# A two-layer local-attention block around full attention, one core: first weights loaded and split by q, k and v, clears moved from POOL to DVE, masks in two steps, q's rearranging read issued before k's writes have landed, and the order of all steps laid out from other numbers

## The reference

```python
x = L0_attn_x
x = x + 0.5 * _L0_ffn_ref(_layernorm(x), ...)   # 2 layers, local attention, 8 heads of 64, window 64
x = x + _L0_attn_ref(_layernorm(x), ...)        # causal attention, 16 heads of 8
x = x + 0.5 * _L0_ffn_ref(_layernorm(x), ...)   # the same two layers and weights again
```

## Time and profile before

| | us |
|---|---|
| median of 3 runs | 1801.35 |
| lowest and highest run | 1790.93 and 1801.44 |
| the profiled execution's own time | 1793.28 |
| its span, first to last instruction | 1791.4 |
| its mean granted TensorE clock, as a share of 2.4 GHz | 0.948 |

### The profile page before, as it was taken

One profiled execution on the slowest core, in us unless ns is written; L12 is line 12 of the kernel. 1 busy time (PEld: TensorE's weight loads), 2 busy tenths in 40 slices (PEclk: granted clock), 3 DMA queues, 4 the chain that ended last, 5 costly groups with the idle time before them and its releaser, 6 DMA issues.

```text
span 1791.4 us, 48412 instructions
## 1 busy us (share of the span) xinstructions
PE 1562.1 (87%) x17754; PEld 1259.1 (70%) x17754; DVE 1448.5 (81%) x2953; ACT 1311.4 (73%) x3846; POOL 1303.5 (73%) x1562
## 2 busy tenths in 40 slices
PE   3789799898988899887989899998889988898987
PEld 3667677666767777766767777776667777677776
DVE  6778789777877889877887998886788897687895
ACT  2588687667677888686779886766578877587885
POOL 7899857368648988687699997732489785469891
PEclk9799999889989999998999998997899999799999
DMA  5001101202010111111010111020210101100000
GB/s 154 16 20 28 42 23 49 92 11 60 13 49 19 25 30 49 33 25 51 24 27 19 25 27 49 21 91 26 71 26 19 52 19 55 51 22 22 19 23 13
DMA packets 49346, 66.75 MB, mean 37 GB/s; under 512 B 8114, under 2 KB 32220, under 8 KB 49116
## 3 DMA queue, kind: packets, MB, share of 16 engines
q1 hardware_dynamic: 49116, 63.66, 12.6%
...
## 4 chain that ended last, share of the span: by engine, by line
POOL 30%; DVE 22%; PE 21%; ACT 11%; DMA 7%; issue 7%; SPq 2%; POOLq 0%; ACTq 0%; DVEq 0%
POOL sums L1198 10%; POOL parts L1188 8%; POOL parts L1202 7%; ACT probs L1264 6%; DVE parts L1568 6%; DMA laid_dram<-halves 4%; PE bank L1640 4%; PE bank L1827 3%; DVE neg_full L1447 3%; DMA stacked_k<-laid_dram 3%; PE bank L1690 2%; PE bank L1788 2%; DVE sums L1575 2%; PE bank L1872 2%; POOL sums L1195 2%
## 5 line engine op out<-in xcount | busy, mean ns | idle before, releaser
L1188 POOL TENSOR_TENSOR parts<-parts 128x256 f32<-128x256 f32 x512 | 382.6, 772 | 136.2 <-DVE parts L1568 134.8
L1198 POOL TENSOR_TENSOR sums<-sums,neg_half 128x8 f32<-128x8 f32 x256 | 434.3, 1696 | 21.3
L1264 ACT ACTIVATE probs<-bank,neg_max 128x128 f32<-128x128 f32 x1024 | 366.2, 406 | 56.4 <-DVE neg_max L1447 54.5
L1568 DVE TENSOR_TENSOR parts<-bank,rope 128x1024 f32<-128x1024 f32 x256 | 309.0, 1216 | 48.3 <-ACT squares L1322 46.7
L1202 POOL TENSOR_TENSOR parts<-parts,sums 128x512 f32<-128x512 f32 x256 | 280.1, 1094 | 37.3 <-POOL sums L1198 0.9
L1264 ACT ACTIVATION_READ_ACCUMULATOR probs<-bank,neg_max 128x1 f32 x1024 | 249.9, 246 | 0.0
L1872 PE MATMUL bank<-ident,parts 128*128 128x128 f32 x1024 | 163.9, 284 | 67.2 <-POOL parts L1202 64.5
L1322 ACT ACTIVATE squares<-bank 128x512 f32<-128x512 f32 x256 | 158.8, 624 | 64.3 <-PE bank L1640 39.2
L1872 PEld LDWEIGHTS bank<-ident,parts 128*128 128x128 f32 x1024 | 117.4, 144 | 99.8 <-issue 71.8
L1640 PE MATMUL bank<-wqkv_hi,h_hi 128*128 128x512 f32 x384 | 179.3, 467 | 4.0 <-ACT q_t L1340 0.8
L1447 DVE TENSOR_REDUCE neg_max<-bank 128x4 f32<-128x512 f32 x256 | 164.2, 681 | 20.6 <-PE bank L1711 19.9
...
## 6 DMA issues: line engine op xcount, KB each, us to landing
between<-val SPq DMA_DIRECT2D x192, 128.0 KB, 2.3
...
stacked_q<-laid_dram SPq DMA_DIRECT2D x16, 512.0 KB, 3.2
stacked_k<-laid_dram SPq DMA_DIRECT2D x16, 512.0 KB, 4.3
...
```

The lines of the kernel that those rows point to most:

```text
L1188: last = nc.gpsimd.tensor_tensor(joined[:, :, dst], joined[:, :, dst], sines[:, :, src], ALU.add)
L1198: nc.gpsimd.tensor_tensor(sums[:, u], sums[:, u], neg_half[:], ALU.pow).then_inc(sems["pool_step"], 1)
L1264: last = nc.scalar.activation(probs[:, u, block:block + wide].rearrange("p b j -> p (b j)"), bank[:, at:at + P * wide], ACT.Exp, bias=neg_ ...
L1568: nc.vector.tensor_tensor(parts[:, u].rearrange("p o (h d) -> p o h d", d=LOCAL_D), bank[:].rearrange("p (o h d) -> p o h d", o=1, d=LOCAL ...
```

## The change

What is computed stays the same. Eight things differ:

- The first projection's weights come as three DMAs (q, k and v columns, `load_qkv`), each with a semaphore; q's stands second in SP's queue, ahead of x of stream 1 and the table. The splits are made for q, k and v apart (512 columns each, for both layers), and `weights_of` lets a `Q` step wait for its own piece only.
- The clears and the ones go from POOL to DVE, ahead of DVE's first statistics; 17 instructions in all, `state`'s old 8 clears aside.
- `MASKS` is two steps: the local masks (the step that stands first) and the full masks, which only full `S` waits for.
- `write` sends q's three DMAs first and then k's, with a semaphore for each, and `lay` issues q's read when q's three have landed, and k's read when k's have.
- The model's durations are changed by some hundredths to a few tenths, `SPREADING` from 9.5 to 14.5 and `WRITING` from 3.6 to 7.5.
- The tables of due times hold other numbers, and a new table `NUDGE` moves single steps.
- Hence each engine's order is another one from the first rows on.
- In that order, ACT's table of functions is loaded 96 times instead of 102.

```diff
-PIECES = [("qkv_hi", 0), ("qkv_lo", 0), ("table", 0), ("w1_scaled", 0), ("w1_hi", 0), ("w1_lo", 0), ("qkv_hi", 1),
-          ("qkv_lo", 1), ("table", 1), ("w1_scaled", 1), ("w1_hi", 1), ("w1_lo", 1), ("wf_scaled", 0), ("wf_hi", 0),
-          ("wf_lo", 0)]
+QKV = ("q", "k", "v")
+PIECES = [(f"{x}_{half}", 0) for x in QKV for half in ("hi", "lo")] + [("table", 0)] + [
+    (f"w1_{x}", 0) for x in ("scaled", "hi", "lo")] + [(f"{x}_{half}", 1) for x in QKV for half in ("hi", "lo")] + [
+    ("table", 1)] + [(f"w1_{x}", 1) for x in ("scaled", "hi", "lo")] + [(f"wf_{x}", 0) for x in ("scaled", "hi", "lo")]
...
-    "SPLIT": [(DVE, 0.85)], "WO": [(PE, 1.75), (DVE, 0.88)],
+    "SPLIT": [(DVE, 0.87)], "WO": [(PE, 1.65), (DVE, 0.88)],
...
-WRITING = 3.6
-SPREADING = 9.5
...
+WRITING = 7.5
+SPREADING = 14.5
...
+STRETCH = 2.1968
+PATIENCE = (0.0, 0.0, 0.144, 0.715)
...
-BEGIN = (1.5, 2.0, 1.0, 5.3)
...
+BEGIN = (2.0, 2.0, 4.5, 1.7)
...
-        return [(POOL, 5.4)]
+        return [(POOL, 3.8 if n else 5.4)]
...
-        return made(("qkv_hi", l), ("qkv_lo", l))
+        x = "v" if kind == "VAL" else QKV[n % 2]
+        return made((f"{x}_hi", l), (f"{x}_lo", l))
...
-                    wait(x, 0, masks)
+                    wait(x, 0, masks[1])
...
-        entry_loaded = sem("entry_loaded")
+        entry_loaded = [sem(f"{x}_loaded") for x in QKV]
...
-        WRITES = 16 * 2 * len(PARTS)
+        WRITES = 16 * len(PARTS)
...
+            def load_qkv(m):
+                sp.dma_start(raw_qkv[:, 0, INNER * m:INNER * (m + 1)],
+                             a["L0_ffn_wqkv"][0, :, INNER * m:INNER * (m + 1)]).then_inc(entry_loaded[m], 16)
+
             load_x(0)
+            load_qkv(0)
+            load_x(1)
             with nc.allow_non_contiguous_dma(reason="bias columns, once"):
 
-                sp.dma_start(rope[:, 1], a["rope"].rearrange("(t p) a b d -> p t a b d", p=P)).then_inc(entry_loaded, 16)
-                sp.dma_start(raw_qkv[:, 0], a["L0_ffn_wqkv"][0]).then_inc(entry_loaded, 16)
+                sp.dma_start(rope[:, 1], a["rope"].rearrange("(t p) a b d -> p t a b d", p=P)).then_inc(scales_loaded, 16)
                 for m, name in enumerate(("L0_ffn_q_scale", "L0_ffn_k_scale")):
                     for l in range(LAYERS):
 
                         src = a[name][l:l + 1].to_broadcast([P, LOCAL_D])
                         sp.dma_start(qk_scale[:, m, l], src).then_inc(scales_loaded, 16)
-                for s in range(1, STREAMS):
+                load_qkv(1)
+                load_qkv(2)
...
-                for part, of in enumerate(PARTS):
-                    for w in range(2):
-                        sp.dma_start(laid[u, w, :, part], halves[SET_OF[step[1:3]]][:, of[w]].bitcast(F32)).then_inc(written[u], 16)
+                for w in range(2):
+                    for part, of in enumerate(PARTS):
+                        sp.dma_start(laid[u, w, :, part], halves[SET_OF[step[1:3]]][:, of[w]].bitcast(F32)).then_inc(written[u][w], 16)
 
             def lay(step):
 
                 u, nth, k = SPREAD_OF[("QF",) + step[1:]], SPREAD_NTH[step[1:]], SET_OF[step[1:3]]
-                sp.wait_ge(written[u], WRITES * nth)
                 sp.wait_ge(spread_pads, 16 * 2 * SPREADS)
                 for w, dst in enumerate((stacked_q, stacked_k)):
+                    sp.wait_ge(written[u][w], WRITES * nth)
...
-            for k in range(SETS):
-                nc.gpsimd.memset(between[k][0:HALF, 0], 0.0)
-            nc.gpsimd.memset(val_full[:], 0.0)
-            nc.gpsimd.memset(spaced[:], 0.0)
-            nc.gpsimd.memset(pads[:], 0.0).then_inc(cleared, 1)
-            n += 1
-            pool.wait_ge(cleared, n)
-            for j in range(P // PAD_D):
-                nc.gpsimd.memset(pads[PAD_D * j:PAD_D * j + 2 * CHUNKS, 1], 1.0).then_inc(cleared, 1)
-                n += 1
-                pool.wait_ge(cleared, n)
-            for k in range(VALUES_FULL):
-                for t in range(TILES):
-                    ones = val_full[:, k, t, 0:FULL_HEADS * VAL_D].rearrange("p (h d) -> p h d", d=VAL_D)[:, :, FULL_D:VAL_D]
-                    last = nc.gpsimd.memset(ones, 1.0)
-            last.then_inc(pads_cleared, 1)
...
+            def make_masks_full():
+                nonlocal n
+                nc.gpsimd.memset(mask_full[:], 0.0)
+                nc.gpsimd.memset(mask_turned[:], 0.0).then_inc(cleared, 1)
+                n += 1
+                pool.wait_ge(cleared, n)
+                for rows in (slice(0, HALF), slice(HALF, P)):
+                    for half in range(2):
+                        select(mask_full[rows, half:half + 1], HALF * half, -1, 1, ALU.is_ge, MASKED)
+                        select(mask_turned[rows, half:half + 1], -HALF * half, 1, -1, ALU.is_ge, MASKED)
+                nc.gpsimd.memset(pool_mark[:], 0.0).then_inc(sems["masked"], 1)
...
-                if what == "qkv_hi":
+                if what[0] in QKV:
+                    x = QKV.index(what[0])
+                    cols = slice(INNER * x, INNER * (x + 1))
+                if what in ("q_hi", "k_hi", "v_hi"):
                     if m == 0:
-                        dve.wait_ge(entry_loaded, 32)
+                        dve.wait_ge(entry_loaded[x], 16)
                     else:
                         dve.wait_ge(w_loaded, 16 * N_WLOADS)
-                    last = nc.vector.tensor_copy(wqkv_hi[:, m], raw_qkv[:, m])
-                if what == "qkv_lo":
-                    last = nc.vector.tensor_tensor(wqkv_lo[:, m], raw_qkv[:, m], wqkv_hi[:, m].bitcast(F32), ALU.subtract)
+                    last = nc.vector.tensor_copy(wqkv_hi[:, m, cols], raw_qkv[:, m, cols])
+                if what in ("q_lo", "k_lo", "v_lo"):
+                    last = nc.vector.tensor_tensor(wqkv_lo[:, m, cols], raw_qkv[:, m, cols], wqkv_hi[:, m, cols].bitcast(F32),
+                                                   ALU.subtract)
                 if what == "table":
                     if m == 0:
-                        dve.wait_ge(entry_loaded, 32)
-                        dve.wait_ge(scales_loaded, 64)
+                        dve.wait_ge(scales_loaded, 80)
...
+            nc.vector.memset(pads[:], 0.0).then_inc(zeroed, 1)
+            nc.vector.memset(val_full[:], 0.0).then_inc(zeroed, 1)
             for s in range(STREAMS):
 
                 nc.vector.memset(state[s][HALF:C, 0:1], 0.0)
+            for k in range(SETS):
+                nc.vector.memset(between[k][0:HALF, 0], 0.0)
+            nc.vector.memset(spaced[:], 0.0)
+            dve.wait_ge(zeroed, 2)
+            for j in range(P // PAD_D):
+                nc.vector.memset(pads[PAD_D * j:PAD_D * j + 2 * CHUNKS, 1], 1.0)
+            for k in range(VALUES_FULL):
+                for t in range(TILES):
+                    ones = val_full[:, k, t, 0:FULL_HEADS * VAL_D].rearrange("p (h d) -> p h d", d=VAL_D)[:, :, FULL_D:VAL_D]
+                    last = nc.vector.memset(ones, 1.0)
+            last.then_inc(pads_cleared, 1)
...
-                if step == FIRST_SCORED:
-                    pe.wait_ge(sems["masked"], 1)
+                if step in FIRST_MASKED:
+                    pe.wait_ge(sems["masked"], NTH["masked"]["MASKS", 0, 0, int(is_full(ph))])
```

100 lines of the change are left out of this document (57 added, 43 removed), and 106 rows, old and new, of tables (DUE, LATER, NUDGE).

## The result

The changed kernel takes 1737.92 us (median of 4 runs, 1734.93 to 1740.84) against 1801.11 (1790.93 to 1801.44, 4 runs): ratio 0.966, interval 0.963 to 0.970, 63 us less. By the profiled executions it is 1791.4 to 1736.1, 55.3 us less. The 8 us between the two lie in the kernel before: its medians beside the other kernels were 1801 to 1803 and single runs went from 1791 to 1808, so its profiled execution (1793.3) was at the low end.

The account below looks back on a forecast made before the run. No engine is full, so the order of work, which must keep PE fed, was taken as the bound. From 1793.3 us, 3.4 for the start and 32 for DRAM waits and clock came off: 1758 us, range 1722 to 1800.

Parts of the forecast that it names:

- main case: Whole kernel: time of 1740 to 1775 us around 1758, chance 0.5.
- all of it reaches the end: Rival: PE's DRAM pauses are true stops and the clock stays up, 1729 us (1715 to 1740), chance 0.12.
- early read: Full attention's q read under k's writes: 1.5 us per stream on six remaining waits, 9 us.
- The waits for DRAM: PE's waits for full attention's q and k through DRAM: 31 of 41.9 us go.
- six streams with 22 to 27 steps: Streams with 22 to 27 PE steps from QF to full S: about 3.4 us wait each, 20 us left.
- The clock behind the waits: PE's slow clock after long DRAM waits: 17 of 22 us go, lower bound 0.
- Two thirds reach the end: Other engines use PE's pauses, so 2/3 x (31 + 17) = 32 us of waits and clock count.
- The start: Kernel's start: first projection matmul at 18.6 us instead of 21.94, 3.4 us earlier.
- The rest of the order: Other moved steps and fewer ACT table loads: set together at 0, with 15 us to either side.
- Others set the pace: Rival: PE only arrives earlier at its waits for POOL and DVE, 1778 us (1770 to 1793), chance 0.25.
- Slower by a denser bunch: Rival: denser full-attention score steps hold PE's clock down, up to 1817 us, chance 0.13.
- The change doing nothing: Rival: clears cost 1.5 times as much and q's early read gives 0, 1770 us; no chance of its own.

Follow-up runs that it names:

- a_order: Changed kernel with old clears, masks, first-weights DMA, write turns and reads behind all six writes, so only the order is new: 1759.0 us, ratio 0.976.
- a_start: Changed kernel with clears back on POOL, all masks together ahead of the first rstd, first weights in one DMA behind the table: 1749.5 us, ratio 0.971.
- b_q: Kernel before with q's three writes first and q's read issued once they landed, then k's; old order: 1784.1 us, ratio 0.990.
- b_start: Kernel before with clears on DVE and full masks behind the second rstd, weights still in one DMA: 1803.2 us, ratio 1.000.
- b_short2: Kernel before with full attention's six writes per stream left out and reads fetching stand-in scores; old order: 1739.7 us, ratio 0.967.
- a_short2: Changed kernel with full attention's six writes per stream left out and reads fetching stand-in scores: 1729.4 us, ratio 0.959.

## Why the prediction was right, and where its terms were off

The time (1738 us) is in the range (1722 to 1800) and on the predicted side, 20 us below the value given. It lies just under the main case (1740 to 1775), in the stretch of the rival "all of it reaches the end" (1715 to 1740), which had 0.12. The fall was forecast as 35 us from 1793.3 and is 55.3 by spans: both terms that it adds, the start's 3.4 us and the waits' 32, were too small. Within the waits one error ran the other way: the early read was put too high, the order's part too low.

**The waits for DRAM, the main term: right in kind, a little small.** The sum had 22 us from the order and 9 from the early read, 31 in all. Measured: 28.5 from the order (a_order) and 5.6 from the early read (a_order to a_start), 34.4 in all. The order's part was mis-sized by the price of the six streams with 22 to 27 steps, 3.4 us each: in a_order four of the six waited, 12.0 us together instead of 20, and a stream with 35 steps another 1.4. The early read was worth 0.84 us a wait (b_q), not 1.5: k's read lands in 3.3 us instead of 4.3 there, but q's takes 5.8 and k's goes out no earlier than before (at 11.6 us in the kernel after).

**The clock behind the waits: right in size, before the two thirds.** I had 17 us for 31 us of waits, 0.55 for each. Measured: 23.8 for 41.9 on the old order, 0.57, and 0.35 on the new one.

**"Two thirds reach the end": the step that failed.** It was taken from two windows, one in which ACT was busy and one in which nothing was. Of 41.9 + 23.8 = 65.7 us, 55.4 reached the end, 0.84. The fraction was near for the waits themselves, of which 31.6 of 41.9 us, 0.75, were idle time saved, since only 10.3 came back at other engines. It was wrong for the clock's part, which it cut too: that part is PE's own busy time, and all of it came off the span. With the measured 1.32 for each of the 34.4 us, the term is 45 us where the sum had 32.

**The start: right in sign, its cost and its reach mis-sized.** First matmul at 19.75, forecast 18.6. The clears on DVE ended at 7.6 us (7.0 forecast), and the statistics ahead of the first rstd at 8.85 (7.8). POOL, not DVE, was last: its first rstd with its `var_eps` took 1.52 us instead of the 0.95 I took, and the selects with their clears 4.9 instead of 4.1. The "4.1 to 10 us" given there as bounds of the clears' cost are the times at which the clears would end; as costs they are 3 to 9 us. On the new order the start was worth 8.9 us (11.6 by medians), not the 2.2 by which the first matmul moved: what it must be compared with is the old start under the new order (25.18), not the old start under the old one. On the old order it was worth nothing (b_start).

**The rest of the order: 0, right.** Without any wait for DRAM the two kernels differ by 10.3 us by medians and 14.1 by spans (b_short2 to a_short2), and the start can account for 8.9 to 11.6 of that. The 0 was set without a row behind it, with 15 us to either side.

Added up by the runs: 45.4 for the waits and 8.9 for the start make 54.3, against 55.3 by spans; at the new order's 1.22 the waits would be 42. The remaining 8 us of the median are that the sum set out from 1793.3, the low execution.

**The rivals.** "All of it reaches the end" (1729 us) had the better mechanism, and the time came out in its stretch. "Others set the pace": POOL and DVE took back 10.3 us, not three quarters. "Slower by a denser bunch": the clock rose. The change doing nothing: ruled out by the ratio. The strict form of the Trainium skill's rule on shared engines, in which the early read gives nothing, held for q's own landing and not for the sum (b_q).

**The signs named.** `stacked_k` at 7.5 us, the first projection matmul at 19.75 and k's read at 3.5: as named. Ahead of that matmul stood POOL, where DVE's table was named, and one wait took 5.0, where none above 4 was named. Clock 0.966 for 0.955 to 0.965, DMA's share of the chain 2% for 3 to 5%: both just beyond the good end.

**Not tried.** b_start had its first projection matmul at 16.94 us, 2.8 us ahead of the kernel after, with the full masks behind the second rstd instead of ahead of it. On the new order, where a start's lead is kept, that may be worth some us; no run shows it. The 7.5 us of waits left are worth 8.5 (a_short2).
